# One more bank for layer F's scores, its first rows copied sooner, and eight product operands on GpSimd instead of six

## What is computed

```python
x = x + A(layernorm(x));  x = x + F(layernorm(x))
# A: 16 heads of width 8; Q = x, K = x@Wk+bk, V = x@Wv+bv (width 32), causal softmax,
#    x + gelu(o) @ Wf + bf
# F: 8 heads of width 64; q = x@w_q, k = x@w_k; gates = sigmoid(x@w_gate), one of 8 experts
#    chosen per row and head; values = gate * (x @ value_experts[chosen]);
#    causal softmax(q*0.125 @ k^T) @ values; out = sum over heads of
#    gate * (out @ output_experts[chosen])
```

## Time and profile before

| what | us |
|---|---|
| median of three runs (1184.46, 1187.67, 1187.96) | 1187.67 |
| the profiled execution, its own time | 1187.65 |
| its span, first to last instruction | 1185.9 |
| PE busy | 1120.6 |
| ACT busy | 938.4 |
| DVE busy | 863.0 |
| POOL busy | 399.6 |

### The profile page before, as it was taken

The page is one execution under the profiler, slowest core; times in us unless marked ns, Lnnn a source line. Parts: engine busy times, 40 slices in busy tenths (PEclk is TensorE's granted clock), DMA queues, the critical chain, the costliest instruction groups (busy, mean ns, idle before and its releaser), DMA issues.

```text
span 1185.9 us, 20345 instructions
## 1 busy us (share of the span) xinstructions
PE 1120.6 (94%) x5846; PEld 649.6 (55%) x5846; DVE 863.0 (73%) x2715; ACT 938.4 (79%) x2639; POOL 399.6 (34%) x652
## 2 busy tenths in 40 slices
PE   5999999999999999999999999999999999999998
PEld 3636754476445754357543775447643585436753
DVE  5835868678785878769687687858787596866844
ACT  3995799858996789967999489976899679995751
POOL 1033324523334334342244332452343532432320
PEclk9999999999999999999999999999999999999999
DMA  6321232022220333003320223202231033201130
GB/s 198 74 76 44 52 111 66 5 64 71 84 56 4 73 92 98 13 15 74 105 72 14 54 53 100 66 4 64 84 88 39 4 82 103 80 2 46 39 73 9
DMA packets 43648, 72.75 MB, mean 61 GB/s; under 512 B 9664, under 2 KB 25408, under 8 KB 43216
## 3 DMA queue, kind: packets, MB, share of 16 engines
q1 hardware_dynamic: 42142, 66.95, 21.2%
q10 hardware_dynamic: 1394, 4.50, 1.5%
HBM read 45.34 MB, written 8.80 MB: 46 GB/s over the span
## 4 chain that ended last, share of the span: by engine, by line
PE 65%; ACT 15%; DVE 9%; issue 5%; DMA 2%; POOL 1%; SPq 1%; ACTq 0%; DVEq 0%; POOLq 0%
PE ps_m L731 14%; PE ps_o L711 10%; ACT masked L956 7%; ACT pt L1007 6%; PE ps_max L608 5%; PE ps_exp L610 3%; PE ps_exp L517 3%; PE ps_m L517 3%; PE ps_exp L519 3%; PE ps_exp L518 3%; PE ps_m L519 3%; PE ps_m L518 3%; PE ps_max L610 3%; PE ps_max L611 3%; PE ps_max L848 2%
## 5 line engine op out<-in xcount | busy, mean ns | idle before, releaser
L956 ACT ACTIVATE masked<-masked,low 128x512 f32<-128x512 f32 (+3 forms) x768 | 423.1, 555 | 48.5 <-DVE low L1349 45.9
L1349 DVE CUSTOM_DVE_ANT_0 masked<-ps_max,mask 128x512 f32<-128x512 f32 (+3 forms) x768 | 349.3, 488 | 128.5 <-PE ps_max L608 77.5
L1216 POOL TENSOR_SCALAR_AFFINE_SELECT pt<-pt 128x256 f32<-128x256 f32 (+2 forms) x384 | 181.7, 475 | 477.5 <-ACT pt L1007 477.1
L1007 ACT ACTIVATE pt<-ps_exp 128x384 f32<-128x384 f32 (+1 forms) x400 | 202.1, 518 | 31.0 <-PE ps_exp L611 25.1
L711 PE MATMUL ps_o<-pt,val 128*32 128x128 f32 (+6 forms) x1536 | 178.8, 445 | 6.1 <-POOL pt L1216 5.4
L731 PE MATMUL ps_m<-at,oe_sb 128*128 128x512 f32 x300 | 154.3, 601 | 1.8 <-DVE at L1400 1.8
L956 ACT ACTIVATION_READ_ACCUMULATOR masked<-masked,low 128x1 f32 x768 | 147.5, 192 | 0.0
L608 PE MATMUL ps_max<-s2k,s1q 72*128 72x512 bf16 (+3 forms) x512 | 121.2, 304 | 18.7 <-DVE low L1349 10.6
L1400 DVE TENSOR_TENSOR at<-osb,hots 128x512 f32<-128x512 f32 x150 | 107.0, 714 | 15.9 <-PE ps_m L731 15.8
L610 PE MATMUL ps_exp<-s1q,s1k 128*128 128x256 f32 (+2 forms) x256 | 97.6, 392 | 10.6 <-DVE val L1540 9.5
L711 PEld LDWEIGHTS ps_o<-pt,val 128*32 128x32 f32 (+1 forms) x1536 | 51.7, 117 | 93.4 <-POOL pt L1216 44.6
(11 more groups left out here) (191 smaller groups left out, 2055.6 us busy)
## 6 DMA issues: line engine op xcount, KB each, us to landing
hots<-hot_d SPq DMA_DIRECT2D x48, 256.0 KB, 4.6
s1q<-parts_q SPq DMA_DIRECT2D x96, 96.0 KB
s2k<-parts_k SPq DMA_DIRECT2D x93, 96.0 KB
s1q<-pt SPq DMA_DIRECT2D x64, 128.0 KB, 2.3
s1k<-pt SPq DMA_DIRECT2D x64, 128.0 KB, 2.3
hots<-hot_d ACTq DMA_DIRECT2D x16, 256.0 KB, 4.8
parts_q<-pt SPq DMA_DIRECT2D x24, 128.0 KB, 2.3
parts_k<-pt SPq DMA_DIRECT2D x24, 128.0 KB, 3.9
```

The lines of the kernel that those rows point to most:

```text
L956: last = nc.scalar.activation(e, e, ACT.Exp, bias=low[:, g % 2, c:c + 1], scale=-1.0, accum_out=den[:, g % 2, c:c + 1])
L1007: nc.scalar.activation(pt[:, (n % 2) * 4 + j, 0:c1 - c0], score_bank(k, u)[:, c0:c1], ACT.Exp).then_inc(exp_done[k].sem, 1)
L1216: nc.gpsimd.affine_select(out=v, in_=v, compare_op=ALU.is_ge, fill=0.0, base=0, pattern=[[0, w], [0, m], [1, P]], channel_multiplier=-1).t ...
L1349: last = v.tensor_tensor_reduce(out=masked[:, u % JUNK, c0:c0 + w], in0=src[:, c0:c0 + w], in1=mask[:, S - w:S], scale=-1.0, scalar=POS, o ...
```

## The change

Five tables and orders change together.

- Layer F's scores use three banks, `(ps_m[0:1] + ps_exp)[u % 3]`. The first three wait for values up to 28, 30 and 31 (before: the first two for 30 and 31), the others for the exponential of the unit three before. The transposes of rows move out of `ps_m[0]`: of layer F's groups 1 to 3 into `ps_m[1]`, of layer A's group 0 from `ps_m[2]` into `ps_m[0]`.
- The first group's rows: the transpose moves from value 27 to value 24, ACT's copy right behind the high half of projection 7.
- In the batches but the last, product 0 moves from unit 15 to unit 16 and the operands behind it are spread one per unit over units 16 to 22.
- POOL makes operands 8 to 15, DVE two fewer.
- In the last batch no product runs before unit 17, then two per unit; the masks of groups 0 and 1 are sent by SP behind the first rows.

```diff
-SCORE_BANKS = {"A": 3, "F": 2}
+SCORE_BANKS = {"A": 3, "F": 3}
-BANK["A", "T", 0] = 2
+BANK.update({("F", "T", g): 1 for g in range(1, GROUPS)})
-NEGATE_AT, TRANSPOSE_AT, COPY_AT = 23, 27, 27
+NEGATE_AT, TRANSPOSE_AT, COPY_WITH = 23, 24, 7
-OUTPUTS_F, OUTPUTS_PRE = 8, 6
+OUTPUTS_F, OUTPUTS_PRE = 8, 8
-STEPS_AT = [("F", 14 + 5 * m // 4) for m in range(OUTPUTS_F)] + [("pre", n) for n in (2, 5, 8, 11)]
+STEPS_AT = [("F", 15 + m if m else 14) for m in range(OUTPUTS_F)] + [("pre", n) for n in (2, 5, 8, 11)]
-    OUTPUTS_LAST["F", (14 + m // 2) if m < E else (18 + 3 * (m - E) // 4)].append(m)
+    OUTPUTS_LAST["F", 16 + m // 2].append(m)
...
-            return ps_exp[u % 2]
+            return (ps_m[0:1] + ps_exp)[u % 3]
...
                 if f + 1 == B:
+                    for p in range(2):
+                        repeat_hots(f, p)
                     maxima_rows("F", f, 1)
-                    for p in range(1, GROUPS):
+                    for p in range(2, GROUPS):
                         repeat_hots(f, p)
...
-                    if k == "A" and exp_done["F"].count(b - 1, UNITS["F"] - 1):
-                        pe.wait_ge(exp_done["F"].sem, exp_done["F"].count(b - 1, UNITS["F"] - 1))
+                    if k == "A" and exp_done["F"].count(b - 1, UNITS["F"] - 2):
+                        pe.wait_ge(exp_done["F"].sem, exp_done["F"].count(b - 1, UNITS["F"] - 2))
...
-                    pe.wait_ge(chosen.sem, chosen.count(b, choices(min(T * E - 1 + u, T * E))))
+                    pe.wait_ge(chosen.sem, chosen.count(b, choices(T * E - (3, 1, 0)[u])))
...
-                                for p in HOTS_AT.get(u, ()):
+                                for p in HOTS_AT.get(u, ()) if b + 1 < B else ():
...
+                    if u == COPY_WITH:
+                        maxima("F", f, 0)
...
-                if n == COPY_AT:
-                    maxima("F", f, 0)
```

## The result

| | median us (runs) | ratio to the kernel before, 95% interval |
|---|---|---|
| before | 1187.5 (11) | |
| changed | 1192.79 (11), 1188.1 to 1196.19 | 1.0044 [1.0032, 1.0056] |

The change makes the kernel slower, by 0.44%, where 5.4 us of gain were forecast. Its runs also spread over 8.1 us, those of before over 4.8, and their times follow the granted clock, which was noted for each execution as a mean over it: 0.998 in the quickest two (1188.10 and 1188.61 us), 0.992 in the slowest two (1195.78 and 1196.19), 0.995 in the median. The profiled execution of the changed kernel took 1191.01 us with a span of 1189.3, 3.4 more than before.

What follows compares the result with a forecast made beforehand. PE, busy 94% of the span, was taken as the bound, with ACT or DVE next. Gains of 2.8 us (first score) and 2.6 (last batch), others zero, summed to 5.4 off 1187.65: 1182.3 us, range 1177.5 to 1186.8.

Steps and rivals of the forecast that it cites:

- The moved products: Seven batches, attention F: product 0 one unit later costs PE nothing; zero, to 0.2 us per batch in favour.
- the first score: Layer F, seven batches: score needs value 28 instead of 30, starts 0.38 us sooner; 0.4 us per batch, 2.8 us.
- the last batch: Last batch: 2.0 us sooner at the first weighting plus 0.6 us later, 2.6 us in all, between 0.5 and 3.5.
- rival 3: Idle time of about 1 us in the experts lowers the clock, 1.7 us per batch: 1198.5 us; chance 0.07.
- the new wait: In the experts, PE waits 0.96 us for DVE's tile before the moved first transposition, delaying values 25 to 31.
- The second term: Last batch, later: 0.6 us gained of PE's 1.36 us wait for the first operand, as the transpose replaces a product.
- POOL's two operands: Seven batches: POOL's stretch ends 2.14 us later, covered by 4.66 us of idle time; zero, within 0.1 us either way.
- Rival 4: POOL's products slow DVE down, making the kernel slower; chance 0.03.
- Rival 1: The new wait in the experts eats the bank's gain in seven batches, as DVE starves: 1185.6 us; chance 0.19.
- Rival 2: PE's waits for maxima in the turn to layer A shrink too, 0.6 us per batch: 1178.1 us; chance 0.11.

Runs made afterwards that it cites:

- e1: Changed kernel with products 0, 1 and 2 back at units 15, 16 and 17 of attention F: 1183.79 us, ratio 0.998.
- e3: Kernel before with only the earlier first rows and the last batch's new order: 1185.73 us, ratio 0.9991.
- e5: Changed kernel with products 0 and 1 both at unit 16, product 2 at 17, units 15 and 18 empty: 1191.96 us, ratio 1.0037.
- e9: Changed kernel with products in old places, rows of ones sent first, and six GpSimd operands instead of eight: 1183.61 us, ratio 0.9975.
- e2: Changed kernel with the first transposition of maxima at value 25 instead of 24: 1191.06 us, ratio 1.0036.
- e7: Changed kernel with unit 15's score computed three times in the first seven batches, as filler: 1188.28 us, ratio 1.0011.
- e11: Changed kernel with products back at units 15 to 17 and the first transposition at value 25: 1184.03 us, ratio 0.9987.

## Why the prediction was wrong, by its steps

**The moved products: the step that failed.** The prediction wrote "Product 0 one unit later takes nothing off PE" and took zero, "covered by PE's scores". Two faults. It read the table for product 0 only, where products 0, 1 and 2 move and the last lands in a unit that had none. And it asked only whether PE waits for an operand, where it should have asked what PE does in the place left empty and what the product displaces where it goes. Measured: 3.7 us of steady loss and 3.9 of clock, 7.6 together, against 0 forecast. This alone is more than the whole forecast gain of 5.4. With the 1.9 us that the first score and the 1.0 that the last batch gave less than forecast, it makes up the 10.5 us between 1182.3 and 1192.79. That sum is an estimate, as its terms come from different rounds.

**The clock, rival 3: right that it can fall, the place wrong.** It was put in the experts, at the new wait. That wait (0.79 us of idle time in the changed kernel's fifth batch, 0.77 to 0.80 over all) stood in all eight batches of eight profiled kernels (the changed one, e1, e3, e5 to e9) with the clock at 1.00 behind it each time. What falls is the clock behind unit 15, three short waits in a row, in some batches only: of the 20 batches with these waits in the profiles of the changed kernel, e2 and e5, three, two of e2 and one of e5. At 1.6 us each the timed 3.9 us would be between two and three falls per execution, an estimate. The wide spread agrees with such falls in varying number: from 0.998 to 0.992 in mean clock is 0.006 of 1190 us, 7.1 us, and the times differ by 7.2 to 8.1. That mean covers the whole execution, so where in it the falls stand is shown only by the profiles and by e7. The one profiled execution of the changed kernel, at 0.997, was among its quicker ones. Why a batch with the same waits falls or not stays open.

**The first score.** It came 40.17 us after the mark, where the working gave 40.18. The new wait was as worked out too: the 0.79 us count from the modelled end of the matmul before; the transposition starts 33.14 us after the mark (forecast 33.16), 0.96 us behind the 32.18 at which PE could have taken the next matmul. "By 709 I count 0.4 us, and from there ACT is nearly full" was too hopeful. The transposition at 44 us waits 0.45 us for DVE, and the lead is then minus 0.08; it comes back to 0.2 to 0.3 through the scores that no longer stand behind exponentials, and then meets the wait for the DMA at 60.2 us, where it is lost in some batches and kept in others. e1's mean of 139.72 against 139.85 before makes 0.9 us of the 2.8.

**The last batch.** Forecast 2.6, measured 1.6 (106.0 to 104.4). The first score at 39.7 us of the batch and the clock at 1.00 came as forecast (1119.71 less 1079.9 is 39.8). The 1.7 us that the prediction adds for the clock there are the 4 us of the earlier trace rows at 0.57 in place of 1.00, 1.72 us; in single us that clock reads 0.63, 0.50, 0.50 and 0.66. But the gain at the first weighting is 0.92 us, not 2.0. PE was 1.5 us ahead before it came to the second transposition, and waited most of that away. GpSimd's gating was taken for the next bound; it is DVE's negated maxima:

```profile
1128.69 0.27 PE L658 MATMUL ps_m<-ident_sb,nm_f 128*16 128x128 f32 x1 [1.33 <-DVE nm_f L1384]
```

The second term was right: 1.36 us of waiting before the first operand became 0.73 before the transposition, and the lead grew to 1.64.

**POOL's two operands.** Right: eight took 8.51 us (1.06 each) and the next mask still came behind 2.78 us of idle time. e9 confirms the zero. Rival 4, which had POOL's products slow DVE down, is out, as no run shows it: beside the eight products DVE's 512-column maxima took 688 ns, against 689 beside six in the earlier trace rows.

**Rivals 1 and 2.** Rival 1 had the right remark that DVE gives on little, but DVE was not starved: its last two copies begin 39.7 us after the mark in both kernels. Rival 2 did not happen: the turn takes 8.93 us of PE's time in 10 (before 8.92), and the waits for maxima grew, from 10.6 to 15.2 us.

Without the moved products the prediction's sum of 5.4 us would have met e1's 0.2%, 2.4 us.

## What to carry to other kernels

When a table of slots is shifted, list all the slots, the one that is left empty as well as the one that is filled: here a product was free in unit 15, where PE otherwise waited 0.67 us for DVE, and cost its full 0.86 us in unit 18. The empty slot beside another short wait cost 3.9 us more than the 3.7 us of the moved product, as the granted clock fell to 0.50 behind it in three of 20 batches; if useful work has to leave, cheap filler in its place is worth a trial (3.9 us in e7). A gain at one wait counts only up to the next point that another engine or a DMA sets, as e11's lead of 1.28 us was 0.03 at the next transposition: follow it there before summing it.

## What the runs showed of the hardware

Behind three waits of 0.27 to 0.47 us within 2.1 us, the granted clock was at half for about 3.4 us (0.57 over the 4 us shown of e2) in three of 20 batches of the changed kernel, e2 and e5, and not in the other 17 with such waits. The one wait of 0.77 to 0.80 us in the experts never did this, nor the 1.12 us of the earlier trace rows, nor the 1.28 to 1.44 us that PE waited in the last batch of nine of the profiles, the changed kernel's 1.33 among them; a wait of 1.51 us (before, last batch) and one of 1.76 us (changed, third batch) were each followed by a fall. So it was not the longest wait alone that decided. And in e7 28 useless matmuls made the changed kernel 3.9 us faster, by ratio, than it is without them.
